# Six rows of maxima and six transposed outputs per batch go through ScalarE's PSUM ring and GpSimd instead of VectorE

## The reference

```python
x = layernorm(x + attn1(x))            # bf16 attention behind a 3-tap convolution
x = layernorm(x + attn2(x, ctx_512))   # the part that changes here
x = layernorm(x + ffn(x))              # routed experts, with a layer norm of its own inside

# attn2, 16 heads of 16, fp32, context of 1024 tokens
q, k, v = x @ Wq + bq, x @ Wk + bk, x @ Wv + bv
y = softmax(causal(q k^T / 4)) v                       # self, 512 x 512 per head
qc, kc, vc = x @ Wcq + bcq, ctx @ Wck + bck, ctx @ Wcv + bcv
y = y + softmax(qc kc^T / 4) vc                        # cross, 512 x 1024 per head
y = y @ Wp + bp
```

## Time and profile before

| | value |
|---|---|
| median of three timed runs | 2283.96 us |
| profiled execution, its own time | 2273.5 us |
| its span | 2271.8 us |
| busy PE / DVE / ACT / POOL | 2139.2 / 1849.8 / 1497.3 / 429.3 us |
| mean granted TensorE clock | 0.967 |

### The profile page before, as it was taken

The page is one execution under the profiler, slowest core; times in us unless marked ns, Lnnn a source line. Parts: engine busy times, 40 slices in busy tenths (PEclk is TensorE's granted clock), DMA queues, the critical chain, the costliest instruction groups (busy, mean ns, idle before and its releaser), DMA issues.

```text
span 2271.8 us, 38997 instructions
## 1 busy us (share of the span) xinstructions
PE 2139.2 (94%) x13138; PEld 932.3 (41%) x13138; DVE 1849.8 (81%) x5065; ACT 1497.3 (66%) x3265; POOL 429.3 (19%) x581
## 2 busy tenths in 40 slices
PE   5999999999999999999999999999999999989993
PEld 2344334543345433453335433454334543345332
DVE  6858969789787889788797897979978798878864
ACT  2935787467864688557894587845887468855761
POOL 3012301132011320123101231023301132002310
PEclk7899999999999999999999999999999999999995
DMA  3700025000430005100170002500033000520000
GB/s 107 136 10 1 1 56 93 11 1 1 102 56 11 1 20 106 34 11 1 29 130 10 1 1 47 112 10 1 1 77 73 10 1 5 107 39 1 1 10 9
DMA packets 250855, 81.78 MB, mean 36 GB/s; under 512 B 236064, under 2 KB 247328, under 8 KB 250656
## 3 DMA queue, kind: packets, MB, share of 16 engines
q1 hardware_dynamic: 250656, 79.29, 17.1%
HBM read 16.35 MB, written 4.19 MB: 9 GB/s over the span
## 4 chain that ended last, share of the span: by engine, by line
PE 72%; DVE 14%; ACT 9%; issue 3%; DMA 1%; SPq 0%; POOL 0%; DVEq 0%; POOLq 0%; ACTq 0%
PE bank L1600 16%; PE bank L1659 13%; PE bank L1650 8%; PE bank L1286 7%; PE bank L1596 5%; ACT work L668 5%; PE bank L1647 4%; PE bank L1553 4%; DVE work L847 3%; PE bank L1416 3%; PE bank L1403 2%; PE bank L1439 2%; DVE top_half L1110 2%; PE bank L1613 1%; PE bank L1697 1%
## 5 line engine op out<-in xcount | busy, mean ns | idle before, releaser
L727 ACT ACTIVATE work<-bank 128x512 f32<-128x512 f32 (+3 forms) x1536 | 725.5, 550 | 341.5 <-PE bank L1647 201.2
L1110 DVE TENSOR_REDUCE top_half<-bank 128x1 f32<-128x512 f32 x1024 | 631.4, 681 | 69.1 <-PE bank L1600 68.1
L1600 PE MATMUL bank<-k_c,q_c 32*128 32x512 f32 x2048 | 568.4, 628 | 0.0
L1650 PE MATMUL bank<-q_c,k_c 32*128 32x512 f32 x2048 | 476.0, 632 | 4.2 <-DVE top_half L1110 3.9
L668 ACT ACTIVATE work<-work,neg 128x512 bf16<-128x512 bf16 x512 | 362.6, 715 | 30.6 <-DVE work L847 29.8
L1659 PE MATMUL bank<-work,v_flat 128*32 128x512 f32 (+3 forms) x3072 | 371.4, 560 | 10.9 <-DVE featA L1129 9.5
L847 DVE TENSOR_SCALAR_CACHE_REDUCE work<-bank 128x512 bf16<-128x512 f32 x512 | 322.3, 686 | 42.9 <-PE bank L1385 33.6
L591 POOL TENSOR_TENSOR featA<-featA,featB 128x512 f32<-128x512 f32 (+3 forms) x232 | 241.8, 1042 | 382.5 <-ACT featB L735 382.5
L1600 PEld LDWEIGHTS bank<-k_c,q_c 32*128 32x128 f32 x2048 | 231.6, 185 | 175.0 <-DVE top_half L1110 126.0
L1107 DVE CUSTOM_DVE_ANT_0 masked<-bank,mask_w 128x384 bf16<-128x384 f32 (+3 forms) x512 | 225.6, 489 | 86.4 <-PE bank L1596 82.2
L1647 PE MATMUL bank<-q_s,k_s 32*128 32x512 f32 (+3 forms) x1024 | 238.7, 474 | 0.0
(11 more groups left out here) (197 smaller groups left out, 2367.2 us busy)
## 6 DMA issues: line engine op xcount, KB each, us to landing
xT_pad<-xT SPq DMA_DIRECT2D x16, 256.0 KB, 3.2
ctx_sb<-ctxT SPq DMA_DIRECT2D x8, 512.0 KB, 3.4
x_res<-x SPq DMA_DIRECT2D x8, 512.0 KB, 4.8
out<-r_sb SPq DMA_DIRECT2D x8, 512.0 KB, 3.1
work<-work SPq DMA_TRANSPOSE x112, 4.4
qk_sb<-qkT SPq DMA_DIRECT2D x1, 512.0 KB, 4.5
pe_sb<-pe_w SPq DMA_DIRECT2D x1, 256.0 KB, 3.5
v_sb<-vT SPq DMA_DIRECT2D x1, 256.0 KB, 6.2
```

What stands on the lines that cost most here:

```text
L727: nc.scalar.activation(pT[:, s % PT_SLOTS, g, q0:S], exp_bank(n)[:, 0:S - q0], ACT.Exp, scale=SCALE).then_inc(pT_ready, 1)
L1110: nc.vector.tensor_reduce(top_half[:, i % 2, g, u // 2, u % 2:u % 2 + 1], scores, AX.X, ALU.max, negate=True).then_inc(slot_out, 1)
L1600: mm(dst, q_c[rows, i, P * t:P * (t + 1)], k_c[rows, i, S * half:S * (half + 1)], start=True, stop=True, tile_position=(GW * g, 0)).then_i ...
L1650: mm(dst, k_c[rows, i, P * u:P * (u + 1)], q_c[rows, i, :], start=True, stop=True, tile_position=(GW * g, 0)).then_inc(sT_mm, 1)
```

## The change

Rows of maxima due in steps 2 to 30 (three self, three cross) and outputs due in steps 7 to 35 (four self, two cross) leave VectorE's ring and enter ScalarE's. The transposes are where they were on TensorE. ScalarE copies the row of maxima to `row_tops` (which lies over `pe_sb`, unused after the start) or the 272 used columns of the output to `o_cols`. GpSimd adds `row_tops` to the stack of queries, or takes the sums to the power of minus one, multiplies, and adds a cross output to `y_sb`. Each of the two buffers is single; ScalarE's next copy waits until GpSimd has read it. The key-major scores of a group now wait for GpSimd's addition. Rows of the last cross group (step 38) and outputs of the last two (step 43 and the end) stay on VectorE.

```diff
+    EARLY_ROWS = 2 * HG - 2
+    EARLY_OUTS = HG + 2
@@ slot_uses
-                order.extend(("rows",) + part for part in rows_behind(s))
-                order.extend(("o",) + part for part in outputs_behind(s))
+                if s >= LATE_STEP:
+                    order.extend(("rows",) + part for part in rows_behind(s))
+                    order.extend(("o",) + part for part in outputs_behind(s))
@@ exp_slot_uses
                 order.extend(("exp", GH * s + g) for g in range(GH))
                 order.extend(("part", p) for p in parts_behind(s))
+                order.extend(("rows", early_rows(*part)) for part in rows_behind(s))
+                order.extend(("o", early_outs(*part)) for part in outputs_behind(s))
@@ GpSimd
+                def add_rows(kind, i):
+                    pool.wait_ge(rows_copied, b * EARLY_ROWS + early_rows(kind, i) + 1)
+                    own_wait(nc.gpsimd)
+                    stack = (q_s if kind == SELF else q_c)[:, i, :]
+                    nc.gpsimd.tensor_tensor(stack, stack, row_tops, ALU.add).then_inc(rows_added, 1)
+                def finish(kind, i):
+                    n = early_outs(kind, i)
+                    pool.wait_ge(o_copied, b * EARLY_OUTS + n + 1)
+                    own_wait(nc.gpsimd)
+                    y = y_sb[:, :, GH * HD * i:GH * HD * (i + 1)].rearrange("p t (g j) -> p t g j", g=GH)
+                    o, sums = o_cols[:, :, :, 0:HD], o_cols[:, :, :, HD]
+                    nc.gpsimd.tensor_tensor(sums, sums, minus_one.unsqueeze(2).broadcast_to([P, NT, GH]), ALU.pow).then_inc(o_step, 1)
+                    pool.wait_ge(o_step, o_steps(b, kind, i) + 1)
+                    own_wait(nc.gpsimd)
+                    over = sums.unsqueeze(3).broadcast_to([P, NT, GH, HD])
+                    if kind == SELF:
+                        nc.gpsimd.tensor_tensor(y, o, over, ALU.mult).then_inc(o_read, 1)
+                    else:
+                        nc.gpsimd.tensor_tensor(o, o, over, ALU.mult).then_inc(o_step, 1)
+                        pool.wait_ge(o_step, o_steps(b, kind, i) + 2)
+                        own_wait(nc.gpsimd)
+                        nc.gpsimd.tensor_tensor(y, y, o, ALU.add).then_inc(o_read, 1)
@@ GpSimd's loop, behind add_part
+                    for part in rows_behind(s):
+                        add_rows(*part)
+                    for part in outputs_behind(s):
+                        finish(*part)
@@ ScalarE, called behind part_out
+                def copy_rows(kind, i):
+                    n = early_rows(kind, i)
+                    if n >= 1:
+                        act.wait_ge(rows_added, b * EARLY_ROWS + n)
+                    act.wait_ge(rows_mm, b * EARLY_ROWS + n + 1)
+                    nc.scalar.copy(row_tops, early_bank("rows", n)).then_inc(rows_copied, 1)
+                def copy_outs(kind, i):
+                    n = early_outs(kind, i)
+                    if n >= 1:
+                        act.wait_ge(o_read, b * EARLY_OUTS + n)
+                    act.wait_ge(o_mm, b * EARLY_OUTS + n + 1)
+                    nc.scalar.copy(o_cols[:], early_bank("o", n).rearrange("p (t g j) -> p t g j", t=NT, g=GH)[:, :, :, 0:HD + 1]).then_inc(o_copied, 1)
@@ VectorE's loop
-                    for part in rows_behind(s):
-                        put_rows(*part)
+                    if s >= LATE_STEP:
+                        for part in rows_behind(s):
+                            put_rows(*part)
@@ TensorE, scoresT of a group's first step
-                        pe.wait_ge(slot_out, base + uses["rows", kind, i] + 1)
+                        if ("rows", kind, i) in uses:
+                            pe.wait_ge(slot_out, base + uses["rows", kind, i] + 1)
+                        else:
+                            pe.wait_ge(rows_added, b * EARLY_ROWS + early_rows(kind, i) + 1)
```

More of the change, by code:

```diff
@@ L425, in exp_bank, with early_bank @@
             return bank[:, exp_ring_bank(exp_uses["exp", n]) if n < FIRST_LATE else LATE_EXP_BANKS[(n - FIRST_LATE) % len(LATE_EXP_BANKS)], :]
+        def early_bank(what, n):
+            return bank[:, exp_ring_bank(exp_uses[what, n]), :]
         def part_bank(p):
-            return bank[:, exp_ring_bank(exp_uses["part", p]), :]
+            return early_bank("part", p)
         def last_exp(at):
@@ L783, in batch @@
                         part_out(p)
+                    if s < LATE_STEP:
+                        for part in rows_behind(s):
+                            copy_rows(*part)
+                        for part in outputs_behind(s):
+                            copy_outs(*part)
             def tail(c):
@@ L1181, in batch @@
                             outputs(j)
-                    for part in rows_behind(s):
-                        put_rows(*part)
+                    if s >= LATE_STEP:
+                        for part in rows_behind(s):
+                            put_rows(*part)
                     if s == ALL_STEPS - NC:
                         do(nc.vector.tensor_tensor(x_res[:], x_res[:], over_tiles(bp_row), ALU.add))
-                    for part in outputs_behind(s):
-                        finish(*part)
+                    if s >= LATE_STEP:
+                        for part in outputs_behind(s):
+                            finish(*part)
                 if ahead:
@@ L1601, in scores, with free_exp_slot @@
                            tile_position=(GW * g, 0)).then_inc(slot_in, 1)
+                def free_exp_slot(use):
+                    if use >= EXP_RING:
+                        what, n = exp_order[use - EXP_RING]
+                        if what == "exp":
+                            pe.wait_ge(pT_ready, b * ALL_SCORES + n + 1)
+                        elif what == "part":
+                            pe.wait_ge(part_copied, b * PARTS + n + 1)
+                        elif what == "rows":
+                            pe.wait_ge(rows_copied, b * EARLY_ROWS + n + 1)
+                        else:
+                            pe.wait_ge(o_copied, b * EARLY_OUTS + n + 1)
                 def max_rows(kind, i):
@@ L1610, in max_rows @@
                         top = top_c[:, i % 2]
-                    dst = free_slot(b, base, uses, uses["rows", kind, i])
+                    early = ("rows", kind, i) not in uses
+                    if early:
+                        free_exp_slot(exp_uses["rows", early_rows(kind, i)])
+                    dst = early_bank("rows", early_rows(kind, i)) if early else free_slot(b, base, uses, uses["rows", kind, i])
                     for t in range(NT):
                         last = nc.tensor.transpose(dst[:, P * t:P * (t + 1)], top[:, t, :], ident[:])
-                    last.then_inc(slot_in, 1)
-                def free_exp_slot(use):
-                    if use >= EXP_RING:
-                        what, n = exp_order[use - EXP_RING]
-                        if what == "exp":
-                            pe.wait_ge(pT_ready, b * ALL_SCORES + n + 1)
-                        else:
-                            pe.wait_ge(part_copied, b * PARTS + n + 1)
+                    last.then_inc(rows_mm if early else slot_in, 1)
                 def scoresT(s, g):
@@ L1694, in o_transpose @@
                         pe.wait_ge(part_added, b * ADDS + adds_before(last_part(kind, i) + 1))
-                    dst = free_slot(b, base, uses, uses["o", kind, i])
+                    early = ("o", kind, i) not in uses
+                    if early:
+                        free_exp_slot(exp_uses["o", early_outs(kind, i)])
+                    dst = early_bank("o", early_outs(kind, i)) if early else free_slot(b, base, uses, uses["o", kind, i])
                     for t in range(NT):
                         last = nc.tensor.transpose(dst[:, P * t:P * (t + 1)], o_rows(kind, i)[:, P * t:P * (t + 1)], ident[:])
-                    last.then_inc(slot_in, 1)
+                    last.then_inc(o_mm if early else slot_in, 1)
                 if ahead:
```

45 lines of the change are left out of this document (31 added, 14 removed).

## The result

| | before | after |
|---|---|---|
| median of 20 timed runs each | 2283.52 us | 2292.59 us |
| ratio, 95% interval | | 1.0033 [1.0020, 1.0047] |
| profiled execution: span, its own time | 2271.8, 2273.5 us | 2286.8, 2288.5 us |
| busy PE / DVE / ACT / POOL | 2139 / 1850 / 1497 / 429 us | 2129 / 1777 / 1536 / 667 us |
| mean granted TensorE clock, profiled execution | 0.967 | 0.959 |

The account below looks back on a forecast made before the run. The prediction took TensorE to set the pace, with VectorE on the path only at the cross outputs of steps 27 and 35. From 2283.96 us, -6.0 - 7.0 + 1.6 + 6.6 = -4.8 gave 2279.2 us, range 2270 to 2292.

Parts of the forecast that it names:

- parts 1 and 2: Six row additions and four self outputs leaving VectorE: worth nothing, since VectorE waits for TensorE there anyway.
- Output of step 27, −6.0 us: Cross output leaving VectorE: the stretched step falls from 3.68 to 2.93 us in 8 batches, -6.0 us.
- Output of step 35, −7.0 us: Cross output leaving VectorE: the last maxima start 0.88 us sooner in 8 batches, -7.0 us.
- Copies on ScalarE, 0: ScalarE's 12 added copies a batch: path free of them, taken as 0, bounds 0 and 0.2 us for 12 x 8.
- Wait for GpSimd's row, +1.6: Steps 22 and 30: TensorE waits 0.1 us for GpSimd's row addition, 16 times, +1.6 us.
- Contention from the power, +6.6: Behind step 35: GpSimd's 2.3 us power delays part 35's addition, so VectorE's L1004 waits 0.94 us in seven batches, +6.6.
- the prediction's own rival: GpSimd's power goes by elements, 3.6 us; L1004 waits 2.2 us; the change turns slower at about 3 us; chance 0.27.
- The rival of a long power: GpSimd's 16-element power takes 3.6 us, delaying VectorE's layer norm behind step 35: sum +4.2, 2288.2 us; chance 0.27.
- the rival of a short power: GpSimd's power takes 1.05 us, part 35 is added before L1004 wants to start: sum -11.4, 2272.6 us; chance 0.27.

Follow-up runs that it names:

- the bank alone: Against the kernel before, six rows of maxima take their bank in ScalarE's ring but VectorE still adds them, without ScalarE copies or GpSimd work: 2293.94 us, 1.0039.
- short power: The changed kernel with GpSimd's power over 16 elements replaced by a multiplication, outputs not normalized; timed against the kernel before: 2282.66 us, ratio 0.9998.
- the mended kernel: Changed kernel; TensorE's fourth score waits for ScalarE's copy, GpSimd finishes step 35's output after part 35's addition and square root; against before: 2276.81 us, 0.9970.

## Why the prediction was wrong

Forecast 2279.2 us and faster; measured 2292.6, slower, just beyond the range (2292). By its steps:

1. **Rows and self outputs "worth nothing" (parts 1 and 2): the step that failed.** In time it was right: step 15 is 6.11 us in both, and with only the outputs moved a batch's steps 0 to 20 still take 68.7 us at clock 1.00. I asked whose time becomes free, saw that VectorE waits for TensorE anyway, and stopped. I did not ask who takes the bank next. It is TensorE's own fourth score; taken early, it changes the rhythm of the engine that sets the pace, and with it the clock. In the mean of the timed runs the clock is 0.0051 lower, by the line of before 10.2 us. The prediction has no term for the clock at all. That the bank is the cause for the rows is shown from both sides: the bank alone gives 1.0039, and one wait takes the rows from 1.0048 to 0.9966. Why a pattern with 0.54 us of standstill loses the clock more often is not shown, nor why the clock is lower with the self outputs moved. The Trainium skill, "TensorE: Matmul & The Clock Gate", section "A second HAM failure mode: psum-queue depth-cycling", tells of a kernel whose cycling through PSUM banks made TensorE idle briefly and often, and whose clock went to and fro between its two levels in consequence. The traces agree in that short pauses and falls go together here, and only in part: step 11 of after has the pause and no fall, and step 7 of before falls without one. A test of pauses of other lengths was not made.
2. **Output of step 27, −6.0 us: right.** Step 29 lost 0.70 us in each of eight batches, −5.6.
3. **Output of step 35, −7.0 us: right in five batches, too large in three.** The last maxima came 0.88 us sooner as said. With the contention taken away (short power) steps 36 to 45 fell from 23.5 us at full clock (what they take with this output on VectorE) by 0.9 in batches 1 to 5, but from 21.6 by only 0.2 in the other three, −4.9 in all. VectorE's chain was read in batch 2. It reaches TensorE through the wait for VectorE's addition L1129 (`featA`) in step 42, and this wait exists five times, in batches 1 to 5. Batch 0 has no third layer norm of a batch before it, 6 and 7 have no convolution there, and TensorE does not wait. Before (us in total, times, longest), then who waited for the same addition with the short power (us in total, times):

```profile
PE bank L1659 <- DVE featA L1129: 9.5, 5, 2.1
...
  PE bank L1751: 5.7, 5
```

4. **Copies on ScalarE, 0: right.** The copy of a row takes 0.585 us, that of an output 0.385.
5. **Wait for GpSimd's row, +1.6: about 0.** (Of this term, the up to 0.1 us for a semaphore stood in no row.) Step 23 grew by 0.09 us and step 31 by 0.19, and the steps behind them gave as much back.
6. **Contention from the power, +6.6: right in its mechanism, mis-sized.** The power takes 2.92 us, not 2.3, and product and sum 0.61 and 0.68. Steps 36 to 45 are longer than with the short power by 1.45 us in five batches and 0.8 in two, +8.8; the medians of after and of the short power differ by 9.9. By the prediction's own rival the change turns slower at a power of about 3 us, and at equal clock it stands close to that point. (That rival's 7 times 2.2 us are 15.4, not 15.6, which moves its time by 0.2 us.)

GpSimd's forms (count; busy us, mean ns; idle before), to be laid beside the earlier trace rows:

```profile
L612 POOL TENSOR_TENSOR featA<-featA,featB 128x512 f32<-128x512 f32 x136 | 173.9, 1278 | 221.4 <-ACT featB L789 220.0 <-POOL featA L612 1.4
L631 POOL TENSOR_TENSOR o_cols<-o_cols,powers 128x16 f32<-128x16 f32 x48 | 140.3, 2922 | 0.0
...
L591 POOL TENSOR_TENSOR ln_r<-ln_r,powers 128x4 f32<-128x4 f32 x32 | 33.7, 1054 | 2.7
...
L619 POOL TENSOR_TENSOR q_c<-q_c,pe_sb 128x512 f32<-128x512 f32 x24 | 30.6, 1275 | 9.4 <-ACT pe_sb L797 9.4
```

Summed: steps 20 to 36 give −5.2 us over the eight batches, steps 36 to 45 about +4 (+0.6 in seven, −0.1 in the first), together −1.2; the line through the runs puts after 2.2 us below before at equal clock. With 10.2 us for the clock (0.0051) this makes +9.0 or +8.0; the medians differ by 9.1, the means by 8.0. The rival of a long power has the right sign for another reason: it covers the contention, and nothing of the 10 us. No case in the prediction held these. The prediction's accounting of the path holds up once the clock is taken out: without the long power the change is at −11.7 us, and the rival of a short power had −11.4; that they lie so near is in part luck, as by the stretches it is −10.0.

What stays open: what in the rhythm brings the clock down, and by what the moved self outputs take part in it.

## What to carry to other kernels

When an operation leaves a ring of banks, ask not only whose time it frees but who takes its bank next, and when; if that is the engine that sets the pace, its rhythm changes though no step is shorter. Read the granted clock of every run beside its time before looking for causes in instructions: here 0.001 was 2 us. Work that goes to GpSimd must be placed by what VectorE does beside it: the power behind part 35 cost less than ahead of it, though it was itself longer there. A chain read in one batch counts for the batches that have the same wait, here five of eight.

## What the runs showed of the hardware

- TensorE's granted clock depended on how its own work was spaced within a step of 6.1 us: with 0.54 us of standstill in the step 0.9566 (rows alone), with the same work spread by a wait 0.9636. Runs of one kernel differ too, from 2272 us at a clock of 0.966 to 2296 us at 0.957 for the kernel before.
- GpSimd's power took 1.054 us for 4 elements and 2.922 for 16. By a straight line through these two forms it is 156 ns an element and 0.43 us besides. A product of 16 elements took 0.225 us.
- The power over 16 elements did not hold VectorE up: in the mended kernel four instructions with two SBUF inputs (L1089, L1010 before) ran beside it in 1.66 us, as before without it. It is itself stretched, from 2.92 to 3.94 us, beside VectorE's instructions with two inputs. The 256-column sum and the 512-column addition do hold VectorE up: beside them the four L1079 of after took 3.13 us in place of 1.67, and beside product and sum in the mended kernel L903 took 0.98 us in place of 0.75. The Trainium skill, "SBUF — State Buffer", section "SBUF: two separate sides", says that whichever of the two engines starts first holds the shared pair of ports for its whole instruction. The trace agrees for long operands, and not for short ones.
